# Attention over short sequences: values ahead of the scores, q and k each in one 512-column pass

## The reference

```python
q = split_heads(einsum('bfe,ed->bfd', x, W_query)); k, v the same with W_key, W_value
scores = einsum('hbqd,hbkd->hbqk', q, k)            # 64 x 64 for each head and sequence
attn = softmax(scores, axis=-1)
out = einsum('hbqk,hbkd->hbqd', attn, v)            # heads put side by side again
return relu(out + einsum('bfe,ed->bfd', x, W_res))
```

## Time and profile before

| what | us |
|---|---|
| median of 3 runs | 1512.87 (1512.8 to 1513.39) |
| the profiled execution | 1513.46 |
| its span, first to last instruction | 1511.7 |
| TensorE busy | 1493.1 (99%) |
| VectorE busy | 1390.5 (92%) |
| ScalarE busy | 1044.5 (69%) |
| GpSimd busy | 872.2 (58%) |

### The profile page before, as it was taken

How to read it: one execution, slowest core, us unless ns; L and a number is a source line. 1 busy time by engine, 2 the same in 40 slices (tenths; PEclk the granted TensorE clock), 3 DMA queues, 4 the chain that set the end, 5 groups by cost and what they waited for, 6 DMA issues and landing times.

```text
span 1511.7 us, 77248 instructions
## 1 busy us (share of the span) xinstructions
PE 1493.1 (99%) x32768; PEld 1405.2 (93%) x32768; DVE 1390.5 (92%) x1793; ACT 1044.5 (69%) x1794; POOL 872.2 (58%) x1548
## 2 busy tenths in 40 slices
PE   7999999999999999999999999999999999999997
PEld 6999999999999999999999999999999999999997
DVE  6999999999999999999999999999999999999996
ACT  4677777777777777777777777777777777777775
POOL 3555555555555555555555555555555555555555
PEclk9999999999999999999999999999999999999999
DMA  3444444444444444444444444444444444444443
GB/s 59 98 85 96 85 96 86 96 86 95 86 96 85 96 85 96 85 96 85 96 86 96 86 96 85 96 86 95 86 96 85 96 85 96 85 96 85 96 86 77
DMA packets 677302, 135.36 MB, mean 90 GB/s; under 512 B 545888, under 2 KB 677216, under 8 KB 677216
## 3 DMA queue, kind: packets, MB, share of 16 engines
q1 hardware_dynamic: 675840, 134.30, 42.9%
q10 hardware_dynamic: 1376, 0.26, 0.1%
HBM read 67.37 MB, written 67.11 MB: 89 GB/s over the span
## 4 chain that ended last, share of the span: by engine, by line
PE 98%; issue 0%; POOL 0%; DVE 0%; ACTq 0%; DMA 0%; ACT 0%; POOLq 0%
PE ps_so L241 18%; PE ps_pt L232 17%; PE ps_so L220 14%; PE ps_qk L198 8%; PE ps_qk L196 8%; PE ps_vr L209 8%; PE ps_qk L197 8%; PE ps_vr L210 8%; PE ps_vr L211 8%; POOL y L154 0%; DMA w_raw<-in_L_rec_W_res_dram 0%; ACTq L334 0%; POOL v_diag L167 0%; DVE row_max L364 0%; ACTq L331 0%
## 5 line engine op out<-in xcount | busy, mean ns | idle before, releaser
L154 POOL TENSOR_TENSOR y<-attn,vr 128x256 f32<-128x256 f32 x512 | 387.4, 779 | 532.4 <-DVE attn L379 512.7
L167 POOL COPY v_diag<-vr 64x264 f32<-64x264 f32 x1024 | 478.7, 467 | 102.9 <-POOL y L154 39.9
L311 ACT ACTIVATE probs_t<-ps_pt 128x512 f32<-128x512 f32 x512 | 307.0, 600 | 160.2 <-PE ps_pt L232 160.1
L364 DVE TENSOR_REDUCE row_max<-ps_so 128x16 f32<-128x1024 f32 x256 | 313.5, 1225 | 69.7 <-PE ps_so L220 69.7
L298 ACT COPY vr<-ps_vr 128x512 f32<-128x512 f32 x512 | 300.6, 587 | 67.3 <-PE ps_vr L211 1.1
L196 PE MATMUL ps_qk<-x_hi,w_hi 128*128 128x256 f32 x1024 | 331.3, 323 | 10.5 <-DVE x_lo L355 9.7
L291 ACT COPY qk<-ps_qk 128x512 f32<-128x512 f32 x512 | 300.6, 587 | 56.6 <-PE ps_qk L198 9.0
L232 PE MATMUL ps_pt<-ident,shifted 128*128 128x128 f32 x2048 | 321.4, 280 | 0.8 <-ACT probs_t L311 0.8
L369 DVE TENSOR_TENSOR shifted<-ps_so,row_max 128x1024 f32<-128x1024 f32 x256 | 313.5, 1224 | 8.8
L241 PE MATMUL ps_so<-v_diag,probs_t 128*64 128x66 f32 x8192 | 296.2, 225 | 1.4 <-DVE attn L379 0.7
L198 PE MATMUL ps_qk<-x_lo,w_hi 128*128 128x256 f32 x1024 | 292.0, 285 | 0.0
(11 more groups left out here) (20 smaller groups left out, 1527.2 us busy)
## 6 DMA issues: line engine op xcount, KB each, us to landing
x_in<-in_r_x_dram SPq DMA_DIRECT2D x1024, 64.0 KB, 2.2
out_dram<-y SPq DMA_DIRECT2D x256, 256.0 KB, 2.5
w_raw<-in_L_rec_W_query_dram ACTq DMA_DIRECT2D x1, 64.0 KB, 2.2
w_raw<-in_L_rec_W_key_dram ACTq DMA_DIRECT2D x1, 64.0 KB, 2.7
w_raw<-in_L_rec_W_value_dram ACTq DMA_DIRECT2D x2, 32.0 KB, 2.7
w_raw<-in_L_rec_W_res_dram ACTq DMA_DIRECT2D x2, 32.0 KB, 2.7
```

The lines of the kernel that those rows point to most:

```text
L154: nc.gpsimd.tensor_tensor(y[:, n % 2, a * HALF:(a + 1) * HALF].rearrange("k t (p j d) -> k j (t p) d", j=2, d=D), attn[:, n % 2, a * HALF: ...
L167: nc.gpsimd.tensor_copy(v_diag[n % 2][j * F:(j + 1) * F, seq, :, :, :, j].rearrange("k a t p d -> k a (t p) d"), vr[n][seq * F:(seq + 1) * ...
L364: nc.vector.reduce_max(row_max[:, :].rearrange("q (h u) -> q h u", h=HEADS), scores, AX_X).then_inc(max_ready, 1)
```

## The change

It makes three edits. `project_qk` projects q of the whole body (512 tokens) in three matmuls of 512 columns, and k in three others, in place of q and k of one half in six matmuls of 256 columns; its third argument now says q or k. The layout of `qk` follows: q and k of all 512 tokens, not two halves with both; `copy_qk` copies the whole bank into one of them. In TensorE's step the values of body i-2 come first, and all 64 scores of body i follow in one run, after a wait for the second copy. The waits for `shifted_ready` and `attn_ready` now stand at the head of the step, ahead of the values.

```diff
--- before.py
+++ after.py
@@ -61,7 +61,7 @@
         y = sb("y", [P, 2, TILES, COLS])
 
 
-        qk = sb("qk", [P, 2, 2, HTOK])
+        qk = sb("qk", [P, 2, TOK])
 
         vr = [sb(f"vr{n}", [P, 2, 4, HALF, PAIRS, VW]) for n in range(RING)]
 
@@ -186,17 +186,14 @@
 
         @block.tensor
         def _(pe):
-            def project_qk(i, n, a):
+            def project_qk(i, n, m):
                 pe.wait_ge(xlo_ready, i + 1)
-                if a == 1 or has(i - 1):
-                    pe.wait_ge(qk_ready, halves(i, a) - 1)
-                tok = slice(a * HTOK, (a + 1) * HTOK)
-                for w in range(2):
-                    ps = ps_qk[:, w * HTOK:(w + 1) * HTOK]
-                    nc.tensor.matmul(ps, w_hi[:, w, :], x_hi[n][:, tok], start=True, stop=False)
-                    nc.tensor.matmul(ps, w_lo[:, w, :], x_hi[n][:, tok], start=False, stop=False)
-                    last = nc.tensor.matmul(ps, w_hi[:, w, :], x_lo[n][:, tok], start=False, stop=True)
-                last.then_inc(qk_done, 1)
+                if m == 1 or has(i - 1):
+                    pe.wait_ge(qk_ready, halves(i, m) - 1)
+                nc.tensor.matmul(ps_qk[:, :], w_hi[:, m, :], x_hi[n][:, :], start=True, stop=False)
+                nc.tensor.matmul(ps_qk[:, :], w_lo[:, m, :], x_hi[n][:, :], start=False, stop=False)
+                nc.tensor.matmul(ps_qk[:, :], w_hi[:, m, :], x_lo[n][:, :], start=False,
+                                 stop=True).then_inc(qk_done, 1)
 
             def project_vr(i, n, a):
                 if a == 1 or has(i - 1):
@@ -215,11 +212,11 @@
                 for u in range(a * HALF, (a + 1) * HALF):
                     for s in range(SEQS):
                         for h in range(HEADS):
-                            b = u % HALF * SEQS + s
+                            tok = slice((u * SEQS + s) * F, (u * SEQS + s + 1) * F)
                             rows, at = slice(h * D, (h + 1) * D), h * BANK + u * F
                             last = nc.tensor.matmul(
-                                ps_so[s * F:(s + 1) * F, at:at + F], qk[rows, a, 0, b * F:(b + 1) * F],
-                                qk[rows, a, 1, b * F:(b + 1) * F], start=True, stop=True)
+                                ps_so[s * F:(s + 1) * F, at:at + F], qk[rows, 0, tok], qk[rows, 1, tok],
+                                start=True, stop=True)
                 return last
 
             def transpose_shifted(i, n, a):
@@ -245,25 +242,21 @@
                 last.then_inc(o_done, 1)
 
             def step(i, n):
-                if has(i):
-                    if has(i - 1):
-                        pe.wait_ge(shifted_ready, i)
-                    if has(i - 3):
-                        pe.wait_ge(attn_ready, i - 2)
-                    pe.wait_ge(qk_ready, halves(i, 0))
-                    score(i, 0)
+                if has(i - 1):
+                    pe.wait_ge(shifted_ready, i)
+                elif not has(i):
+                    pe.wait_ge(shifted_ready, N)
+                if has(i - 3):
+                    pe.wait_ge(attn_ready, i - 2)
                 if has(i - 2):
                     pe.wait_ge(pt_ready, halves(i - 2, 1))
                     pe.wait_ge(v_moved, (i - 2) * 4 + 4)
-                    if not has(i):
-                        pe.wait_ge(shifted_ready, N)
-                        pe.wait_ge(attn_ready, i - 2)
                     weigh_values(i - 2, n)
                 if has(i):
                     pe.wait_ge(qk_ready, halves(i, 1))
+                    score(i, 0)
                     score(i, 1).then_inc(s_done, 1)
                 if has(i - 1):
-                    pe.wait_ge(shifted_ready, i)
                     transpose_shifted(i - 1, n + 1, 0)
                 if has(i + 1):
                     project_qk(i + 1, (n + 1) % RING, 0)
@@ -284,11 +277,11 @@
 
         @block.scalar
         def _(act):
-            def copy_qk(i, a):
-                act.wait_ge(qk_done, halves(i, a))
+            def copy_qk(i, m):
+                act.wait_ge(qk_done, halves(i, m))
                 if has(i - 1):
                     act.wait_ge(s_done, i)
-                nc.scalar.copy(qk[:, a].rearrange("p w t -> p (w t)"), ps_qk[:, :]).then_inc(qk_ready, 1)
+                nc.scalar.copy(qk[:, m], ps_qk[:, :]).then_inc(qk_ready, 1)
 
             def copy_vr(i, n, a):
                 act.wait_ge(vr_done, halves(i, a))
```

## The result

The changed kernel takes 1504.14 us (median of 4 runs, 1503.88 to 1504.75), the kernel before 1513.13: ratio 0.994, 95% interval 0.9929 to 0.9952. It is faster by 9 us, where 76 were forecast.

What follows compares the result with a forecast made beforehand. TensorE was the bound at 5.815 us a body; gains of 0.14 and 0.18 left 5.495, VectorE 5.50, plus 0.01: 5.51. Over 254 bodies 77.5 less, 1.4 more at the ends: 1437 us; range 1429 to 1470 (forecast 1429 to 1448).

Steps and rivals of the forecast that it cites:

- Scores in one run: TensorE's 64 score matmuls in one run were to take 0.66 us in place of 0.84, gaining 0.18 a body.
- Rival B: The merged score run is starved by instruction supply in later bodies as in body 1: 1479 us, chance 0.10.
- The wide passes: TensorE's q and k in six 512-column matmuls of 0.215 us, in place of twelve of 256, gain 0.14 a body.
- Rival C: Columns set the price and each 512-column matmul for q and k costs 0.24 us: about 1468 us, chance 0.10.
- The ends: Start and end of the kernel cost 1.4 us more, from late first scores and possible fetch stalls in unrolled steps.
- What bounds the kernel: TensorE sets the pace at 5.815 us a body before the change, with VectorE a quarter of a microsecond behind.
- VectorE's ring: VectorE's own work in a body takes 5.50 us, row_max starting 0.08 before x_lo ends; at worst 5.61.
- Rival D: On VectorE, row_max does not overlap x_lo: 5.61 us a body, about 1462 us, chance 0.10.
- the ring through both: The cycle through VectorE and TensorE, from row_max through attn, values and scores to the next row_max, takes 5.45 us.
- The new waits: Waits on the copies of q and k and on exp cost nothing; 0.01 us a body charged where x_lo meets attn.
- Faster: The whole kernel gets faster by over 0.2%, chance 0.92.

Runs made afterwards that it cites:

- The run in the loop: 64 fp32 score-shaped pairs in a short loop on TensorE alone, added behind the changed kernel's last body; the run took 0.91 us, the kernel's time not compared.
- the longer loop: Changed kernel with four rounds of longer score-shaped runs and matmuls of several widths on TensorE alone behind it, refetching its instructions; its time is not compared.
- the bf16 kernel: Changed kernel with q and k copied to bf16 and scores taken from these, halving the score pairs and dropping their low parts: 1431.82 us, ratio 0.9463.

## Why the prediction was wrong, point by point

- **Scores in one run.** This is the step that failed: "One run of 64 needs that once: 0.42 + 4 x 0.06 = 0.66 in place of 0.84". It is 0.84. The pace of a run's first 32 pairs was carried on past them, where a step of 0.15 and 8 ns a pair wait; what the saved change of shape gives, they take. That the two come out equal to the hundredth has no shown cause. The row against it was there and I explained it away by an instruction fetch that fell beside it. The run in the loop, without fetches, has the same 0.91. Rival B was this outcome, with a chance of 0.10; the fetch that it named as the cause was not it.
- **The wide passes.** The term 1.43 - 6 x 0.215 = 0.14 was mis-sized: it is 0.03. The start of the run, where 256 columns take 0.21, could not tell a floor from a rate: a limit of 0.445 ns a column, (0.233 - 0.119) / 256, lies above a column at full clock (0.417) and below one at half (0.833), so it shows only at full clock. (That the start ran at the 1.2 GHz level was read off that duration; the profile prints a granted clock of 1.00 there. The rows of the longer loop at a granted 0.50 bear the reading out.) Rival C had 0.24.
- **B and C together** were no case of mine; they were kept as alternatives, and both came. 5.813 less 0.03, and less 0.01 in sum at v, the residual and the scores, is 5.774; why v and the residual got slightly shorter no run tells. That put the time 34 us outside the range.
- **The ends** were charged with 1.4 us. The body's gain over 254 bodies is 9.9, the spans differ by 1511.7 - 1502.1 = 9.6, so they cost some 0.3.
- **What bounds the kernel**, TensorE with VectorE a quarter of a microsecond behind: right, before and after.
- **VectorE's ring** of 5.50: right, by the bf16 kernel, where 242 bodies lie in 1330 us, 5.496 each. Rival D falls. The 5.45 of the ring through both was not tested.
- **The new waits**: right. None has time of its own in the changed kernel, and the kernel with the wide passes alone shows what k's copy would have cost.
- **Faster**: right in sign alone: 9 us in place of 76, and they come from the wide passes with the new order hiding k's copy.

What stays open is why the edge lies at 32 pairs. It goes by the number of instruction pairs, the same in fp32 and bf16 and with 16 and 64 columns, and one 512-column matmul in between resets it. That fits instructions queued ahead of TensorE being used up. The Trainium skill, page "TensorE: Matmul & The Clock Gate", gives the engine in its opening table a queue of 64 instructions, which would be 32 pairs; the rows agree with that number. No row shows the queue itself, so the cause is argued and only the edge is shown.

## What to carry to other kernels

A pace read off a short burst of small matmuls holds for a burst of that length; before merging bursts, look for a longer one in the trace, and take its row over an explanation. On TensorE, small matmuls are priced by how many instruction pairs come in a row (here 32 were cheap) as much as by columns. A rate seen at half clock is no evidence for full clock, and where two rivals each take one term of a sum, price them together as well.

## What the runs showed of the hardware

- An fp32 matmul of the score's or the value's shape is two pairs in the profile, a bf16 one is one: the 32 "matmuls" of a score half are 16 calls in the code. Transposes and fp32r matmuls are one.
- fp32r costs 0.119 us for 256 columns, 0.176 for 384 and 0.233 for 512, with TensorE alone and at full clock: 0.445 ns a column and 5 ns fit all three. bf16 costs 0.109 and 0.216. The rows with three fp32r widths in a row are these, 18 matmuls in 1541.20 - 1537.94 = 3.26 us, of which 6 x (0.233 + 0.176 + 0.119) are 3.17:

```profile
1537.94 3.43 PE L293 MATMUL ps_qk<-x_hi,w_hi 128*128 128x512 f32 x18
```

- Half of the values costs 0.62 and all of them 1.09, so for these two lengths a run of another shape has some 0.15 of entry and exit beside its pairs.
